# A Mamba, attention and expert layer: GpSimd makes u*B for three of sixteen state indices

## The reference

```python
xz = x @ W_in.T;  x_ssm, z = split(xz)
x_ssm = silu(causal_conv(x_ssm, 4 taps) + conv_b)
proj = x_ssm @ W_x.T                       # 33 columns: B (16), C (16), one for dt
dt = softplus(proj[..., -1:] * W_dt + b_dt)
A = -exp(A_log)                            # (di, 16)
h[t] = exp(dt[t] * A) * h[t-1] + (x_ssm[t] * dt[t]) * B[t]     # state (di, 16)
y[t] = sum_n h[t, :, n] * C[t, n] + x_ssm[t] * D
out = (y * silu(z)) @ W_out.T
x = layernorm(x + out)
```

## Time and profile before

| | us |
|---|---|
| median of 3 runs | 1689.43 |
| lowest and highest | 1685.65, 1699.95 |
| the profiled execution, its own time | 1687.66 |
| its span, first to last instruction | 1685.9 |
| from the first take_y (chunk 1) to the last (after chunk 15) | 873.04 |

### The profile page before, as it was taken

The page is one execution under the profiler, slowest core; times in us unless marked ns, Lnnn a source line. Parts: engine busy times, 40 slices in busy tenths (PEclk is TensorE's granted clock), DMA queues, the critical chain, the costliest instruction groups (busy, mean ns, idle before and its releaser), DMA issues. The chain is left out here.

```text
span 1685.9 us, 22891 instructions
## 1 busy us (share of the span) xinstructions
PE 1361.7 (81%) x7612; PEld 959.2 (57%) x7612; DVE 1466.5 (87%) x2714; ACT 1113.7 (66%) x2452; POOL 902.0 (54%) x659
## 2 busy tenths in 40 slices
PE   7687778778877877787877879988998899889880
PEld 5566566656666666566665645456545654464460
DVE  5999999999999999999999956597859785978678
ACT  5877887788788778877887523337633763375570
POOL 1778877787878788788778600002800280028015
PEclk9889889888988998998898989999999999999995
DMA  7200210221022022102111021100020001000000
GB/s 237 67 26 32 69 68 3 70 70 42 28 70 70 1 69 70 58 13 70 64 33 56 13 86 46 40 1 1 11 70 1 1 14 38 1 1 1 25 1 25
DMA packets 38040, 70.02 MB, mean 42 GB/s; under 512 B 3553, under 2 KB 31682, under 8 KB 33698
## 3 DMA queue, kind: packets, MB, share of 16 engines
q1 hardware_dynamic: 37922, 68.56, 12.1%
HBM read 59.90 MB, written 8.65 MB: 41 GB/s over the span
## 5 line engine op out<-in xcount | busy, mean ns | idle before, releaser
L900 POOL TENSOR_TENSOR state_c<-state,c_area 128x1024 f32<-128x1024 f32 x256 | 601.7, 2361 | 168.2 <-DVE state L970 149.0
L970 DVE TENSOR_TENSOR_SCAN state<-decay,ps 128x512 f32<-128x512 f32 x512 | 620.5, 1212 | 0.0
L686 ACT ACTIVATE decay<-step_area,negA 128x255 f32<-128x255 f32 x1024 | 432.5, 496 | 0.5 <-DVE step_area L1049 0.5
L945 DVE TENSOR_TENSOR ps<-step_area,ps 128x512 f32<-128x512 f32 x512 | 349.7, 683 | 10.6 <-PE ps L368 8.5
L1562 POOL TENSOR_TENSOR big<-big,g_sb 128x1024 f32<-128x1024 f32 x29 | 80.8, 2788 | 504.8 <-ACT big L1462 502.8
L384 PE MATMUL ps<-ident_sb,state_c 128*128 128x128 f32 x2048 | 294.8, 292 | 12.6 <-POOL state_c L900 12.5
L384 PEld LDWEIGHTS ps<-ident_sb,state_c 128*128 128x128 f32 x2048 | 255.5, 151 | 40.7 <-POOL state_c L900 23.0
L368 PE MATMUL ps<-parts,sel_bc_sb 96*128 96x256 bf16 x256 | 75.4, 295 | 95.8 <-DVE ps L961 75.8
L1421 PE MATMUL ps<-w_sb,hT 128*128 128x256 f32 x512 | 119.9, 388 | 2.4 <-ACT hT L1531 1.9
L1386 PE MATMUL ps<-w_sb,weights 128*128 128x512 f32 x256 | 121.0, 608 | 0.1
L1650 DVE BATCH_NORM_STATS2 stats<-big 128x6 f32<-128x256 f32 x256 | 88.4, 414 | 28.1 <-ACT big L1536 20.2
(11 more groups left out here) (210 smaller groups left out, 2386.6 us busy)
## 6 DMA issues: line engine op xcount, KB each, us to landing
c_area<-c_scratch SPq DMA_DIRECT2D x32, 1024.0 KB, 6.4
weights<-in_xT SPq DMA_DIRECT2D x16, 256.0 KB, 3.0
res<-in_x SPq DMA_DIRECT2D x16, 256.0 KB, 2.8
x_scratch<-res SPq DMA_DIRECT2D x16, 256.0 KB, 8.2
weights<-x_scratch SPq DMA_DIRECT2D x4, 1024.0 KB, 7.8
xa<-x_scratch SPq DMA_DIRECT2D x4, 1024.0 KB, 5.4
...
```

Of the source, the lines that this page charges most:

```text
L686: nc.scalar.activation(decay[:, n % RING, j, 1:], dt_sb[:, i[1] % 2, j, 1:], ACT.Exp, scale=negA[:, j * NS + n:j * NS + n + 1]).then_inc(s ...
L900: nc.gpsimd.tensor_tensor(state_c[:, n % RING, :, :], state[:, n % RING, :, :], c_bc[:, q, n, :].unsqueeze(1).to_broadcast([P, CT, TC]), A ...
L945: nc.vector.tensor_tensor(bu_ps[m % 3][:, :].rearrange("p (j n) -> p j n", j=2), u_sb[:, i[1] % 2, 2 * h:2 * h + 2, :], b_ps[n % 2][:, 0:T ...
L970: nc.vector.tensor_tensor_scan(state[:, n % RING, pair, :].rearrange("p j n -> p (j n)"), decay[:, n % RING, pair, :].rearrange("p j n -> ...
```

## The change

Of the 16 state indices, three (`OFF` = 3, 6 and 9) no longer have their u*B made by VectorE. A DMA broadcasts their B rows through DRAM into `b_bc`, GpSimd multiplies them with u into an SBUF ring of two tiles `ub` and adds the carry (`product_b`), and ScalarE writes their decay into the PSUM ring `bu_ps` (`psum_decay`), with a zero first column copied in for each half. The scan of such an index takes its decay from PSUM and its u*B from SBUF. On ScalarE the decay of an index n of `OFF` is written after that of n+1, and each half waits until its PSUM bank has been scanned (`bu_free`: half (n, 0) for scan (n-2, 1), half (n, 1) for scan (n-1, 0)).

The B rows of the other 13 are broadcast by one fp32 matmul each, from the projected rows themselves (16x256) with a column of the identity, broadcast, as weights. The three-part split goes away: `split`, `next_lead` and the second half of `copies`, and `sel_bc` and `sel_p` with their loads. The norm chain of chunk i-2 uses fused multiply-and-add (nine instead of ten tiny GpSimd operations, without the constants in `coef`) and stands later: `spreads` at place 5 for 3, `variance` 3 for 2, `guess` 8 for 6, `newton` 6 for 4, `normalise` 13 for 9. The expert weights w1 and w2 (1 MB each) are loaded at the start of the second part and no longer ahead of it.

```diff
+        OFF, APART = (3, 6, 9), 3
+        KEPT = [n for n in range(NS) if n not in OFF]
...
+        def bu_free(i, n, h):
+            p = USERS.index((n, h))
+            return scanned(i if p >= 3 else shift(i, -1), *USERS[p - 3])
...
+                if not is_first(k):
+                    sp.wait_ge(s_ub, at(k, 2 * NO))
+                rows = bc_dram[bass.ds(at(k, BC, OFF[0]), APART * NO), :].rearrange("(a s) n -> a s n", s=APART)
+                sp.dma_start(b_bc[:, :, :], rows[:, 0, :].partition_broadcast(P)).then_inc(s_bb, 16)
                 sp.wait_ge(s_y, count)
...
+                if n in OFF:
+                    return
                 if n == 0:
-                    pe.wait_ge(s_split, at(i, 2, 2))
...
-                nc.tensor.matmul(b_ps[n % 2][:, 0:TC], sel_bc_sb[:, n, :], parts[:, i[1] % 2, :], start=True, stop=True)\
+                nc.tensor.matmul(b_ps[n % 2][:, 0:TC], ident_sb[0:NS, n:n + 1].to_broadcast([NS, P]), proj[0:NS, i[1] % 2, :],
+                                 start=True, stop=True)\
...
+                if n in KEPT:
+                    for j in range(CT):
+                        nc.scalar.activation(decay_tile(i, n)[:, j, 1:], dt_sb[:, i[1] % 2, j, 1:], ACT.Exp,
+                                             scale=negA[:, j * NS + n:j * NS + n + 1]).then_inc(s_decay, 1)
+                if n - 1 in OFF:
+                    psum_decay(i, n - 1)
 
+            def psum_decay(i, n):
+
+                for h in range(2):
+                    act.wait_ge(s_scan, bu_free(i, n, h))
+                    bank = bu_bank(i, n, h)[:, :].rearrange("p (j n) -> p j n", j=2)
+                    nc.scalar.activation(bank[:, :, 0], zeros[:, :], ACT.Copy)
+                    for e in range(2):
+                        j = 2 * h + e
+                        nc.scalar.activation(bank[:, e, 1:], dt_sb[:, i[1] % 2, j, 1:], ACT.Exp,
+                                             scale=negA[:, j * NS + n:j * NS + n + 1]).then_inc(s_decay, 1)
...
-                    work += [(0, lambda: take_sum(old, 0)), (1, lambda: take_sum(old, 1)), (3, lambda: spreads(old)), (6, lambda: guess(old)),
-                             (9, lambda: normalise(old))]
+                    work += [(0, lambda: take_sum(old, 0)), (1, lambda: take_sum(old, 1)), (5, lambda: spreads(old)), (8, lambda: guess(old)),
+                             (13, lambda: normalise(old))]
...
+            def product_b(i, n):
+
+                c, later = OFF.index(n), i[1] % CPB
+                if c == 0:
+                    pool.wait_ge(s_u, at(i, 1, 1))
+                    pool.wait_ge(s_bb, at(i, 16, 16))
...
+                nc.gpsimd.tensor_tensor(tile, u_sb[:, i[1] % 2, :, :], b_bc[:, c, :].unsqueeze(1).to_broadcast([P, CT, TC]),
+                                        ALU.mult).then_inc(s_ub, 1 if later else 2)
...
+                work += [(2, lambda: product_b(i, OFF[1])), (5, lambda: product_b(i, OFF[2]))]
+                if prepare:
+                    work.append((15, lambda: product_b(k, OFF[0])))
...
+                if n in OFF:
+                    if h == 0:
+                        dve.wait_ge(s_ub, at(i, 2 * NO, 2 * OFF.index(n) + 2))
+                    a, b = bu_bank(i, n, h)[:, :], flat(ub_tile(i, n))
```

More of the change, by code:

```diff
@@ L43, with mamba_block @@
 TG = 4
-def mamba_block(nc, x, xT, w_in, w_x, w_out, par, ident_sb, ident, sel_bc, sel_p, c_dram, x1, ahead, s_ahead, ps, early, late, shared,
+def mamba_block(nc, x, xT, w_in, w_x, w_out, par, ident_sb, ident, bc_dram, x1, ahead, s_ahead, ps, early, late, shared,
                 w, ctxT):
@@ L64, in mamba_block @@
         SKIP_AT = 8
+        OFF, APART = (3, 6, 9), 3
+        KEPT = [n for n in range(NS) if n not in OFF]
+        NO, NK = len(OFF), len(KEPT)
+        USERS = [(n, h) for n in range(NS) for h in range(2)]
+        EMIT = []
+        for n in range(NS):
+            if n in KEPT:
+                EMIT.append(n)
+            if n - 1 in OFF:
+                EMIT.append(n - 1)
         w_ssm, diag_w, xi, w_gate, xT_sb, w_x_sb = (early[n] for n in ("w_ssm", "diag_w", "xi", "w_gate", "xT", "w_x"))
@@ L86, in mamba_block @@
         inject = sb("inject", [P, NS, CT])
-        rest = sb("rest", [PARTS * BC, TC])
         proj = sb("proj", [PROJ, 2, TC])
-        lead = sb("lead", [PARTS * BC, TC], BF16)
-        parts = sb("parts", [PARTS * BC, 2, TC], BF16)
         yg = sb("yg", [P, CTT, DI])
@@ L148, in mamba_block @@
         s_bu = sem("s_bu")
+        s_ub = sem("s_ub")
+        s_bb = sem("s_bb")
         s_scan = sem("s_scan")
@@ L186, in shift, with rank, scanned, bu_bank @@
             return (i[0], i[1] + n)
+        def rank(n):
+            return sum(m < n for m in KEPT)
+        def scanned(i, n, h):
+            return at(i, 2 * NS, 2 * RING + 2 * n + h + 1)
+        def bu_bank(i, n, h):
+            return bu_ps[at(i, len(USERS), USERS.index((n, h))) % 3]
+        def bu_free(i, n, h):
+            p = USERS.index((n, h))
+            return scanned(i if p >= 3 else shift(i, -1), *USERS[p - 3])
+        def decay_tile(i, n):
+            return decay[:, at(i, NK, rank(n)) % RING, :, :]
+        def ub_tile(i, n):
+            return ub[:, at(i, NO, OFF.index(n)) % 2, :, :]
         def is_first(i):
@@ L622, in first_decay @@
                 nc.scalar.activation(first_dA[:, k[1] % 2, :, :], first_dA[:, k[1] % 2, :, :], ACT.Exp).then_inc(s_dA, 1)
-            def next_lead(k):
-                act.wait_ge(s_split, at(k, 2, 1))
-                nc.scalar.activation(lead[:, :], rest[:, :], ACT.Identity,
-                                     scale=par_sb[0:PARTS * BC, MASKS + 1:MASKS + 2]).then_inc(s_lead, 1)
             def terms(k, j):
@@ L905, in turn @@
                             what()
+            nc.gpsimd.memset(zeros[:, :], 0.0)
             nc.gpsimd.memset(decay[:, :, :, 0], 0.0).then_inc(s_zero, 1)
-            for c, value in enumerate((0.5, 1.5, 1.0 / DM, LN_EPS, -1.0 / DM)):
-                nc.gpsimd.memset(coef[:, c, :], value).then_inc(s_coef, 1)
-            half, one_half, per_dm, eps, minus_per_dm = (coef[:, c, :] for c in range(5))
             pool.sem_inc(s_sum, RING)
@@ L917, in _ @@
             injections(first, 0, NS - RING)
+            product_b(first, OFF[0])
             turns(pool, turn)
@@ L1043, in _ @@
                                         ALU.mult, ALU.add).then_inc(s_v, 1)
-            dve.wait_ge(s_lead, 1)
-            nc.vector.tensor_tensor(parts[:, 0, :], rest[:, :], lead[:, :], ALU.subtract).then_inc(s_split, 1)
             dve.wait_ge(s_v, CT)
@@ L1063, in _, with attn_ffn_block @@
             round_neg(1)
-def attn_ffn_block(nc, x1, ctxT, ident_sb, w, ps, late, shared, g2, be2, bias_rows, before, out):
+def attn_ffn_block(nc, x1, ctxT, ident_sb, w, w1, w2, ps, late, shared, g2, be2, bias_rows, before, out):
     U = G * NL
@@ L1915, in decoder_block @@
             ahead.append((w[name][tuple(slice(None) for _ in shape)], source))
-        mamba_block(nc, x, xT, w_in, w_x, w_out, par, ident_sb, ident, sel_bc, sel_p, c_dram, x1, ahead, s_ahead, ps, early, late,
+        mamba_block(nc, x, xT, w_in, w_x, w_out, par, ident_sb, ident, bc_dram, x1, ahead, s_ahead, ps, early, late,
                     shared, w, ctxT)
-        attn_ffn_block(nc, x1, ctxT, ident_sb, w, ps, late, shared, g2, be2, bias_rows, before, out)
+        attn_ffn_block(nc, x1, ctxT, ident_sb, w, channels(w1), channels(w2), ps, late, shared, g2, be2, bias_rows, before, out)
 def _constants():
-    one = 0x3F80
-    sel_bc = np.zeros((PARTS * BC, NS, P), np.uint16)
-    for q in range(PARTS):
-        for n in range(NS):
-            sel_bc[BC * q + n, n, :] = one
-    sel_p = np.zeros((PROJ, P), np.float32)
-    sel_p[PROJ - 1] = 1
     before = np.tri(E, k=-1, dtype=np.float32).reshape(E * E)
-    return dict(ident=np.eye(P, dtype=np.float32), sel_bc=sel_bc, sel_p=sel_p, before=before)
+    return dict(ident=np.eye(P, dtype=np.float32), before=before)
 def _layout(inputs):
```

170 lines of the change are left out of this document (78 added, 92 removed).

## The result

The changed kernel takes 1743.95 us (median of 4 runs, 1743.43 to 1744.36), the kernel before 1694.69 (4 runs). The ratio is 1.031, with a 95% interval of 1.027 to 1.034: slower by 3%, where 1687 us was forecast, and outside the range of 1640 to 1712. The profiled execution's span is 1742.6 us, 56.7 more than before.

What follows compares the result with a forecast made beforehand. VectorE and the loop over ScalarE, GpSimd and TensorE were taken as level bounds; +5 (13 chunks), -2 (chunk 0), -1 (chunk 1) and -3 (chunk 15) made -1 on 1687.66 us, named as 1687 us, range 1640 to 1712.

Steps and rivals of the forecast that it cites:

- Two bounds stood level: Before the change, VectorE's work (58.1 us per chunk) and the loop over ScalarE, GpSimd and TensorE (58.2) both bound the kernel.
- The step that failed: TensorE, fp32 rows elsewhere in the chunk: 13 x 0.3 = 4 us, hidden beside VectorE's work in 13 us idle.
- The upper bound of +0.4 a row: TensorE behind softplus: high bound on an fp32 row's extra time, giving 12.9 us to the next index 0's B row.
- the +0.7 of the sum itself: TensorE behind softplus: B row of 15 at the low clock, transposes of 11 starting at 6.6 us instead of 5.9.
- Behind softplus: From softplus's end to the next index 0's B row: 12.4 us instead of 11.5, with bounds 12.0 and 12.9.
- the forecast of 58.9: The new loop per chunk: 44.6 + 12.4 + 1.9 = 58.9 us, against 58.2 before.
- the earlier z tile: ScalarE ahead of silus: second z tile taken 1.5 to 2 us earlier, at about 26.8 us into the chunk.
- "All nothing": Start, w1 and w2 loads ahead of the attention, and later normalise delaying a store and reload of res: no cost.
- In the last chunk I forecast -3: Chunk 15 prepares no next chunk, so up to 3.9 us of VectorE's saving could show; -3 us taken.
- The slower one: Rival: low TensorE clock lasts through second out_tile and in_proj, 1.5 us more per chunk, 1707 us; chance 0.16.
- The two faster ones: Rivals: loop shortens at full TensorE clock, 1660 us, chance 0.22; VectorE's saving in full, 1627 us, chance 0.12.

Runs made afterwards that it cites:

- off_36: The changed kernel with OFF = (3, 6), index 9 back on VectorE, fp32 rows kept: 1708.1 us, 1.012 of the kernel before.
- split_off_369: The changed kernel with its fp32 rows undone (three-part bf16 split put back), OFF = (3, 6, 9) kept: 1696.9 us, 1.003 of the kernel before.
- the fastest kernel: The changed kernel with the three-part bf16 split back, OFF = (3, 6) and normalise at place 15: 1667.7 us, 0.985 of the kernel before.
- fill_project: The changed kernel with six unread fp32 matmuls added in TensorE's wait for silu ahead of project: 1751.5 us, 1.037 of the kernel before.

## Why the prediction was wrong

**What was right.** Two bounds stood level, and taking work from VectorE alone gave nothing. With the rows in bf16, the chunk went as the forecast had it: second z tile taken by 26.8 us (26.8 predicted), table load at 30.2 (30.4), softplus ended at 44.8 (44.6), VectorE idle for 3.8 us per chunk at B rows (4.5), and 1693 us against 1687. GpSimd's products took 2.36 us each, and VectorE waited for none of them; the scan with its operands changed over took 1210 ns (0 to +0.1 us had been allowed on 1.21).

**The step that failed** is the one that said "Elsewhere the fp32 rows lie beside VectorE's work, 13 x 0.3 = 4 us on a TensorE that is idle for 58 - 45 = 13 in a chunk". Two things were wrong in it. The size: 0.4 us at full clock and 0.8 at the low one were taken from `out_tile`, a chain of equal matmuls; a row by itself, between other operations, took 0.63 and 1.15, so +0.52 and +0.96 against a bf16 row, where the sum had +0.3 for a row elsewhere and +0.7 for the row of 15 at the low clock. The upper bound of +0.4 a row that I gave with it lay below both measured values, and below the +0.7 of the sum itself. The Trainium skill ("FP8 and Floating Point Precision", "TensorE Precision Notes") says that true fp32 takes four passes through the array; the four matmuls of `out_tile` at 457.36 took 1.73 us, 0.43 each, which agrees with four times the bf16 row's 0.11, and the lone row adds 0.2 to that; where these 0.2 us go was not measured. The place: I set all rows but those of 15 and 0 against TensorE's idle time in the chunk as a whole. That idle time lies ahead of project and y_back. Between the input projection and the second z tile there is almost none (9.43 us busy of 10 from 406.41 on), and TensorE hardly waited there any more for VectorE, which the change itself had put ahead (idle time ahead of all B rows 16.5 us, before 95.8); so each row pushed the z tile, and with it ScalarE's whole run up to softplus. In chunk 6 the second z tile was taken by 28.3 us, 1.5 later than the forecast of 26.8, and softplus ended at 45.9 instead of 44.6, where the sum had nothing for these rows. In four other chunks the z tile came 1.6 us later still.

**Behind softplus** the forecast was 12.4 us to the next B row, at most 12.9; chunk 6 took 13.3. The B row of 15 met the low clock (1.15 us), and `out_tile` took 3.62 us instead of 3.25. So of the 2.2 us by which chunk 6 missed the forecast of 58.9, 1.3 come from ahead of softplus and 0.9 from behind it. Where the clock was full there, as in chunk 7, VectorE had already lost the time at the B rows of 11 and 13, 2.6 us each.

**ScalarE.** Exps into PSUM took 459 ns against 496 into SBUF: the whole PSUM decay came to the 1.9 us that I had taken. That it stands on the loop was in the sum, but I let it pass as balanced by the earlier z tile; with the tile late it was a loss of 1.7 us a chunk (off_36).

**"All nothing"** held for the part behind the last take_y. It failed at the start, +5.7 us, 4.3 of them gone with bf16 rows (94.91 for the first take_y). In the last chunk I forecast -3; it became 8.2 us longer (57.6 before, from this row of the kernel before to the last take_y; 65.9 after):

```profile
908.92 1.21 DVE L933 TENSOR_TENSOR yg<-ps,gate 128x1024 f32<-128x1024 f32 x1
```

In the changed kernel TensorE waited 3.83 us there for a copy that stands behind a PSUM decay on ScalarE, but since the kernel without such decays lost more there (70.6 us), this isn't the whole cause, and no run settles it. The fp32 rows are the smaller part of it: with the split put back (split_off_369) the last interval is 62.5 us, 3.4 less, and VectorE's stall of 8.94 us still stands there with 8.66, in the fastest kernel too with 8.65, where the kernel before had 1.80 and 0.93 at its B rows. The later norm chain was no free move: 18 us for `normalise` between places 13 and 15, and some 9 for the whole chain between its old places and its new ones.

**The rivals.** The slower one had the right sign and the wrong mechanism. The low clock did not spread: the mean granted clock was 0.915 against 0.917, the first `out_tile` took over 3 us in 8 of 14 chunks before as after, and the second one ran at the full clock (1.89 us) in all 14; fill_project adds that the full clock at `project` gives nothing. The two faster ones did not come even without the fp32 rows: with bf16 rows the second z tile was taken by 26.8 us, as in the forecast and no earlier, and the kernel took 1693 us.

**Sum.** 5.7 at the start + 42.7 in 14 chunks + 8.2 in the last = 56.6 us, of 56.7. Of the whole, the fp32 rows explain 47 us (split_off_369), 32 of them shown to be TensorE's time; what makes up the other 15 stays open.
